# Four engines with instruction orders of their own, tile 1's attention moved into tile 0's FFN, and the last two tiles' attention run as a pair

## What is computed

```python
x = x + linear_attention(layernorm(x))   # 16 heads, silu feature map
x = x + ternary_ffn(layernorm(x))        # 256 -> 1024 (gated silu), 1024 -> 1024 gelu, twice, 1024 -> 256
x = x + softmax_attention(layernorm(x))  # one head of width 256, 512 x 512 scores a tile
x = x + tanh(layernorm(x) @ W @ A1 @ A2 + bias)
```

## Time and profile before

| | |
|---|---|
| median of 3 runs | 2118.21 us (2117.63 to 2120.3) |
| the profiled execution's own time | 2119.35 us |
| its span, first to last instruction | 2117.6 us |
| PE busy | 2008.2 us, 95% of the span, 15484 matmuls |
| PEld, DVE, ACT, POOL busy | 91%, 56%, 40%, 18% |
| granted TensorE clock, mean | 0.991 |

### The profile page before, as it was taken

One profiled execution on the slowest core, in us unless ns is written; L12 is line 12 of the kernel. 1 busy time (PEld: TensorE's weight loads), 2 busy tenths in 40 slices (PEclk: granted clock), 3 DMA queues, 4 the chain that ended last, 5 costly groups with the idle time before them and its releaser, 6 DMA issues.

```text
span 2117.6 us, 37472 instructions
## 1 busy us (share of the span) xinstructions
PE 2008.2 (95%) x15484; PEld 1926.5 (91%) x15484; DVE 1189.6 (56%) x2881; ACT 836.7 (40%) x1538; POOL 373.9 (18%) x347
## 2 busy tenths in 40 slices
PE   6899999999999999999999999999999999999985
PEld 5798999989999998999989999998999989999985
DVE  4555656456565555656456565555656456565544
ACT  2334434344333444434344333444434344333422
POOL 1111211112121011211112121011211112121011
PEclk9999999999999999999999999999999999999997
DMA  9500000000000000000000000000000000000000
GB/s 361 184 3 2 21 1 1 21 1 21 1 21 1 1 21 1 21 1 1 21 1 21 1 21 2 1 21 1 21 1 1 21 1 11 1 11 1 1 11 10
DMA packets 24421, 46.01 MB, mean 22 GB/s; under 512 B 1152, under 2 KB 21376, under 8 KB 24064
## 3 DMA queue, kind: packets, MB, share of 16 engines
q1 hardware_dynamic: 24240, 43.41, 5.8%
HBM read 35.02 MB, written 19.92 MB: 26 GB/s over the span
## 4 chain that ended last, share of the span: by engine, by line
PE 79%; DVE 8%; ACT 5%; DMA 3%; issue 2%; POOL 1%; SPq 0%; DVEq 0%; ACTq 0%; POOLq 0%
PE ffn_fill L857 41%; PE att_fill L818 21%; PE ffn_fill L818 8%; PE ffn_fill L915 6%; PE att_fill L873 2%; DVE whole L585 2%; ACT L786 2%; DMA scratch_h2T<-in_h2T 1%; ACT whole L756 1%; PE att_fill L991 1%; ACT kv_b L786 1%; DVE st L520 1%; DMA scratch_h1T<-in_h1T 1%; POOL act_lo L503 1%; DVE sm L661 1%
## 5 line engine op out<-in xcount | busy, mean ns | idle before, releaser
L857 PE MATMUL ffn_fill<-act_hi,h 128*128 128x256 f32 x4096 | 989.7, 284 | 8.8 <-DVE flag L722 3.3
L857 PE MATMUL ffn_fill<-act_lo,h 128*128 128x256 f32 x4096 | 980.6, 281 | 0.0
L857 PEld LDWEIGHTS ffn_fill<-act_hi,h 128*128 128x128 f32 x4096 | 773.5, 189 | 16.2 <-POOL act_lo L503 6.3
L857 PEld LDWEIGHTS ffn_fill<-act_lo,h 128*128 128x128 f32 x4096 | 774.6, 189 | 3.7
L594 DVE CAST act_hi<-whole 128x512 fp32r<-128x512 f32 x256 | 109.2, 426 | 618.6 <-ACT whole L756 618.6
L756 ACT ACTIVATE whole<-ffn_fill,scales 128x256 f32<-128x256 f32 x512 | 215.1, 471 | 493.0 <-PE ffn_fill L857 491.9
L818 PE MATMUL ffn_fill<-half_hi,w 128*128 128x256 f32 x1024 | 251.4, 287 | 12.8 <-DVE whole L585 9.4
L818 PE MATMUL ffn_fill<-half_lo,w 128*128 128x256 f32 x1024 | 247.2, 282 | 0.0
L503 POOL TENSOR_TENSOR act_lo<-whole,act_hi 128x512 fp32r<-128x512 f32 x128 | 166.8, 1303 | 368.2 <-DVE act_hi L590 367.6
L490 POOL TENSOR_TENSOR rstd_B<-var_eps_B,minus_half 128x2 f32<-128x2 f32 x32 | 22.6, 707 | 1176.7 <-DVE var_eps_B L527 1176.7
L818 PEld LDWEIGHTS ffn_fill<-half_hi,w 128*128 128x128 f32 x1024 | 194.7, 190 | 15.8 <-issue 15.8
(11 more groups left out here) (156 smaller groups left out, 3161.6 us busy)
## 6 DMA issues: line engine op xcount, KB each, us to landing
x<-in_L_attn_x SPq DMA_DIRECT2D x16, 512.0 KB, 3.5
out<-x SPq DMA_DIRECT2D x16, 512.0 KB, 3.0
h<-scratch_h1T SPq DMA_DIRECT2D x1, 4096.0 KB, 18.2
h<-scratch_h2T SPq DMA_DIRECT2D x1, 4096.0 KB, 14.4
w<-scratch_w1T SPq DMA_DIRECT2D x1, 1024.0 KB, 16.0
w<-scratch_w2T SPq DMA_DIRECT2D x1, 1024.0 KB, 19.3
w<-scratch_w3T SPq DMA_DIRECT2D x1, 1024.0 KB, 6.4
rows<-in_rows SPq DMA_DIRECT2D x1, 640.0 KB, 5.7
```

The lines of the kernel that those rows point to most:

```text
L857: last = pe.matmul(two(bank)[:, o, :], view(w), view(moving[:, k, :]), start=k == 0 and o == 0 and half == 0, stop=k == KH - 1 and half == ...
```

## The change

Each engine gets an order of its own for each part, in `PE_ORDERS`, `DVE_ORDERS`, `ACT_ORDERS` and `POOL_ORDERS`; the semaphores' values still come from the one list, from copies of the counters taken at each step. On PE a step can be cut in two pieces (`G0a`, `G0b`), with other steps between them; a piece `a` of a hidden layer does the first half of its contraction. `to_fill` in the U steps is asked for one bank at a time.

`PROLOGUE` loses FOLD, TAKE, WIDE and the checks beyond the first matrix. In `FIRST`, tile 1's whole linear attention and the folding stand inside tile 0's first FFN half. `LAST` and `TAIL` become `END`: tile 15's FFN, nearly alone, and then the softmax attention of tiles 14 (`c:`) and 15 (`d:`) side by side. The `d:` steps have their own buffers, laid over the FFN weights that are done with, own semaphores (`late_...`), and use the `ffn_fill` ring.

On SP, w1 and w2 are bounced first, then tile 1 is loaded, then the raw matrices, which lie no longer in the x slots 1 to 3 and `whole` but in slots 2 and 3 and a buffer `staged`; h1 is bounced behind the landing of w1 and w2; w3 is bounced and landed ahead of h2; each large matrix lands in two DMAs with a semaphore for each half. The stores and loads of x in the steady part are as before, with one semaphore for each slot. The matmuls, and the operations of the other engines, are the same in number and shape.

```diff
 PROLOGUE = steps_from("""
-    a:AST a:ANO a:AB PREP a:T a:AKV0 SCALE a:AKV1 a:AKV2 a:AKV3 a:AS a:AQ a:AM a:AO FOLD0 WIDE
-    n:BST0 n:BNO0 TAKE0 n:BT0 FOLD1 LOOK00 TAKE1 LOOK01 CHECK0 LOOK10 LOOK11""")
+    a:AST a:ANO a:AB PREP a:T a:AKV0 SCALE a:AKV1 a:AKV2 a:AKV3 a:AS a:AQ a:AM LOOK00 a:AO
+    n:BST0 LOOK01 n:BNO0 n:BT0 CHECK0""")
...
+PE_ORDERS = {
+    "FIRST": order_from("""
+    U0 U1 a:T U2a a:AKV0 a:AKV1 a:AKV2 U2b a:AKV3 U3 CHECK1 a:AS a:AQ a:AM FOLD0 G0a a:AOa G0b a:AOb G1 G2
+    FOLD1 CHECK2 G3 H0 H1 H2a CHECK3 H2b H3 BT1 W0 U0 U1 U2 U3 G0 G1 G2 G3 H0 H1 H2 H3 n:BT0 W1"""),
+    "BODY": order_from("""
+    U0 U1 U2 U3a c:T U3b G0a c:CV c:CZ G0b G1a c:CS0 G1b G2 c:CP0 c:CS1 G3a c:CS2 G3b c:CO0 c:CP1 H0a c:CS3
+    H0b c:CO1 c:CP2 H1a c:CO2 c:CP3 H1b H2 c:CO3 H3 BT1 W0 U0a c:T U0b U1 c:CF a:T U2 U3a a:AKV0 a:AKV1
+    a:AKV2 a:AKV3 U3b G0a a:AS a:AQa G0b a:AQb G1 G2 a:AM G3 a:AOa H0 a:AOb H1 H2 H3 n:BT0 W1"""),
+    "END": order_from("""
+    U0 U1 U2 U3 G0 G1 G2 G3 H0 H1 H2 H3 BT1 W0 U0 U1 U2 U3 G0 G1 G2 G3 H0 H1 c:T H2 H3 W1 c:CV c:CZ d:T
+    c:CS0 c:CS1 d:CV c:CP0 d:CZa c:CO0 c:CP1 d:CZb c:CO1 c:CS2 c:CS3 d:CS0 c:CP2 d:CS1 c:CO2 d:CP0 c:CP3
+    c:CO3 d:CO0 d:CS2 d:CP1 d:CO1 d:CS3 d:CP2 d:CO2 d:CP3 c:T d:CO3 c:CF d:T d:CF"""),
+}
+DVE_ORDERS = {
...
+    "BODY": order_from("""
+    c:CST U0 c:CNO U1 c:T U2 U3 c:CQ c:CV c:CZ c:CS0 G0 c:CP0 c:CS1 c:CS2 G1 G2 c:CO0 G3 c:CP1 c:CS3 c:CO1
+    c:CP2 c:CO2 BST1 H0 c:CP3 H1 BNO1 a:AST c:CO3 H2 c:DST H3 BT1 c:DNO W0 c:T a:ANO c:CF U0 a:T U1 a:AKV0
+    a:AKV1 a:AKV2 a:AKV3 U2 U3 a:AS G0 a:AQ a:AM G1 G2 G3 a:AO n:BST0 n:BNO0 H0 H1 H2 H3 n:BT0 W1"""),
...
+ACT_ORDERS = {
...
+    "BODY": order_from("""
+    U0 U1 U2 c:T U3 c:CV c:CZ G0 c:CS0 G1 G2 c:CP0 c:CS1 c:CS2 G3 c:CP1 c:CS3 c:CP2 H0 c:CP3 H1 H2 H3 BT1
+    c:T U0 U1 c:CF a:T U2 a:AKV0 U3 a:AKV1 a:AKV2 a:AKV3 a:AQ G0 a:AM G1 G2 G3 H0 H1 H2 H3 n:BT0"""),
...
+POOL_ORDERS = {
...
+    "BODY": order_from("""
+    c:CST U0 U1 c:CB U2 U3 BST1 a:AST c:DST U0 c:CF U1 a:AB U2 U3 n:BST0"""),
...
+            bounce(0, "w1T", "w2T")
+            sp.dma_start(x[:, 1], x_in[1]).then_inc(x_loaded[1], 16)
...
+            land(0, 0, "w1T", w12[:, 0])
+            land(0, 1, "w2T", w12[:, 1])
+            bounce(1, "h1T")
+            bounce(3, "w3T")
+            sp.wait_ge(w_bounced[1], 16)
+            land(1, 0, "h1T", h1[:, :KH // 2])
+            land(1, 1, "h1T", h1[:, KH // 2:])
+            bounce(2, "h2T")
+            sp.wait_ge(w_bounced[3], 16)
+            land(3, 0, "w3T", w3[:])
+            sp.wait_ge(w_bounced[2], 16)
+            land(2, 0, "h2T", h2[:, :KH // 2])
+            land(2, 1, "h2T", h2[:, KH // 2:])
```

More of the change, by code:

```diff
@@ L21 @@
+from collections import namedtuple
 from contextlib import ExitStack
@@ new lines @@
+    n:BST0 LOOK01 n:BNO0 n:BT0 CHECK0""")
+FIRST = steps_from("""
+    U0 a:AST U1 a:ANO U2 a:T U3 LOOK10 a:AB a:AKV0 a:AKV1 LOOK11 a:AKV2 LOOK12 a:AKV3 LOOK13 CHECK1 a:AS a:AQ
+    G0 a:AM FOLD0 G1 TAKE0 a:AO WIDE G2 LOOK20 LOOK21 FOLD1 TAKE1 G3 LOOK22 LOOK23 CHECK2 LOOK30
+    H0 CHECK3 H1 BST1 BNO1 H2 H3 BT1 W0 U0 U1 U2 U3 G0 G1 G2 G3 H0 H1 n:BST0 n:BNO0 H2 H3 n:BT0 W1""")
+BODY = PLAN
+END = steps_from("""
+    U0 U1 U2 U3 G0 G1 G2 G3 H0 H1 BST1 BNO1 H2 H3 BT1 W0 U0 U1 U2 U3 G0 G1 G2 G3 H0 H1 c:CST c:CNO H2 c:T H3 c:CB W1
+    d:CST c:CQ c:CV c:CZ d:CNO d:T c:CS0 c:CS1 d:CB d:CQ d:CV c:CP0 c:CO0 d:CZ c:CP1 c:CO1 c:CS2 c:CS3
+    d:CS0 d:CS1 c:CP2 c:CO2 c:CP3 c:CO3 d:CP0 d:CO0 c:DST d:CS2 d:CP1 d:CO1 c:DNO d:CS3 c:T d:CP2 d:CO2 d:CP3 d:CO3
+    d:DST c:CF d:DNO d:T d:CF""")
@@ new lines @@
+DVE_ORDERS = {
+    "FIRST": order_from("""
+    a:AST U0 a:ANO U1 a:T LOOK10 LOOK11 a:AKV0 a:AKV1 a:AKV2 LOOK12 LOOK13 a:AKV3 U2 CHECK1 a:AS U3 a:AQ
+    a:AM TAKE0 LOOK20 LOOK21 G0 a:AO WIDE G1 LOOK22 LOOK23 G2 TAKE1 CHECK2 LOOK30 G3 H0 H1 CHECK3 BST1 BNO1
+    H2 H3 BT1 W0 n:BST0 U0 U1 U2 U3 n:BNO0 G0 G1 G2 G3 H0 H1 H2 H3 n:BT0 W1"""),
+    "BODY": order_from("""
+    c:CST U0 c:CNO U1 c:T U2 U3 c:CQ c:CV c:CZ c:CS0 G0 c:CP0 c:CS1 c:CS2 G1 G2 c:CO0 G3 c:CP1 c:CS3 c:CO1
+    c:CP2 c:CO2 BST1 H0 c:CP3 H1 BNO1 a:AST c:CO3 H2 c:DST H3 BT1 c:DNO W0 c:T a:ANO c:CF U0 a:T U1 a:AKV0
+    a:AKV1 a:AKV2 a:AKV3 U2 U3 a:AS G0 a:AQ a:AM G1 G2 G3 a:AO n:BST0 n:BNO0 H0 H1 H2 H3 n:BT0 W1"""),
+    "END": order_from("""
+    U0 U1 U2 U3 G0 G1 G2 G3 H0 H1 BST1 H2 BNO1 H3 BT1 W0 U0 U1 U2 U3 G0 G1 G2 c:CST G3 c:CNO c:T H0 c:CQ H1
+    H2 H3 W1 d:CST c:CV d:CNO c:CZ d:T c:CS0 c:CS1 d:CQ c:CP0 d:CV c:CO0 c:CP1 d:CZ c:CO1 c:CS2 c:CS3 d:CS0
+    c:CP2 d:CS1 c:CO2 c:CP3 d:CP0 c:CO3 d:CO0 d:CS2 d:CP1 c:DST d:CO1 d:CS3 c:DNO d:CP2 d:CO2 d:CP3 c:T
+    d:CO3 d:DST c:CF d:DNO d:T d:CF"""),
+}
@@ L287, in build @@
         raw_wq = gated[:, 0]
[L288 to L295, removed]
+        raw_q, raw_k, raw_v, raw_out = (x[:, 2 + n // 2, 2 * (n % 2):2 * (n % 2) + 2, :] for n in range(4))
@@ L561, in part @@
+                    wait_apart(dve, taken[own.ring][b], n)
+                    statistics(c, own, x[:, slots[who]], stage_of(step), NB)
                 elif kind == "BST":
@@ L843, in ffn_products, with halves, begun, hidden @@
                     emit(lambda ap: ap)
-            def hidden(c, layer, weights, src, j):
-                bank, done = to_fill(pe, c, "ffn_fill", 0)
+            def halves(piece, n):
+                return range(n // 2 if piece == "b" else 0, n // 2 if piece == "a" else n)
+            def begun(c, ring, piece):
+                if piece != "b":
+                    return to_fill(pe, c, ring, 0)
+                b, _ = c.bank(ring, 0)
+                return banks[ring][b], full[ring][b]
+            def hidden(c, layer, weights, src, j, piece):
+                bank, done = begun(c, "ffn_fill", piece)
                 def emit(view):
-                    for k in range(KH):
+                    for k in halves(piece, KH):
                         if j == 0 and k % 2 == 0:
@@ L964, in part @@
                     for k in range(KD):
[L965 to L967 removed]
+                        wait_taken(pe, c, own.ring, c.ago(own.ring, "T", 0, who == "d") + k)
+                    for g in halves(piece, 2):
+                        bank, done = to_fill(pe, c, own.ring, g)
                         for b in range(2):
```

445 lines of the change are left out of this document (243 added, 202 removed).

## The result

The changed kernel takes 2039.08 us, median of 4 runs (2038.69 to 2043.08), against 2119.05 (2117.63 to 2120.3) for the kernel before: the ratio is 0.9627, 95% interval 0.961 to 0.9644. The forecast was 2047. The profiled execution took 2039.22 us, with a span of 2037.5, 80.1 less than before.

A forecast was written before the change was run, and what follows sets the result against it. PE was taken to bound the body, 97% busy at full clock yet losing 6.2 us a pass. Savings of 5.5 (front) + 56 (body) + 10 (end) = 71.5 us gave 2047, range 2027 to 2066 (2027 to 2080 with rivals).

The forecast's parts named there:

- the mechanism: Body: one list serves four engines, so each consumer stands right behind its producer on PE; 6.2 us a pass not work.
- The body: The 14 steady passes: each falls from 126.98 to 123.0 us by new orders, saving 56 us.
- The walk: Following one body pass step by step from U0: 120.8 + 1.6 + 0.65 = 123.0 us, margins 0.2 and 1.5.
- Every gap named as gone: Body PE gaps to vanish: CP1 1.48 us, CO0 0.9, one after CF 0.5, one of 0.36 at the exp chain.
- H0a or U2b: Tightest places in a body pass: margins 1.5 us at H0a, 0.2 at U2b; a new gap there means wrong.
- The normalisation beside POOL: CNO on DVE beside U0's low part on POOL: 2.34 us used; 2.8 at worst, making the body 6 us longer.
- The front: Before the body: moved DMAs and folding start U0 at about 39 and the body at 162, gaining 5.5 us.
- The end: After the body: tile 15's FFN 86 us, then two softmax attentions 76 us; 162 in all, gaining 10 us.
- New waits for old: Rival, body: DVE's margins are absent, PE waits 1 to 3 us a pass; pass about 125.3, time 2079; chance 0.17.
- The clock in the end: Rival, last stage: PE runs its 45 us at 1.2 GHz throughout, time 2080; chance 0.04.
- Slower: Rival, body: DVE holds G1 and G2 behind c:CS2, ACT stops, PE loses 5.6 us a pass; 2125; chance 0.05.
- no change: Rival, whole kernel: the ends lose the body's gain, or gaps are replaced one for one; 2118; chance 0.02.

The follow-up runs named there:

- Experiment 1: Changed kernel, but in the 14 body passes all four engines walk the one list again; front and end stay changed: 2100.62 us.
- experiment 3: Changed kernel, but in PE's body order G3 stands ahead of CP0, CS1, CS2, CO0, CP1: 2055.11 us, one run.
- experiment 8: Changed kernel, but DVE does U1 ahead of normalisation CNO, and PE does U3 whole, then c:T: 2046.22 us, one run.
- Experiment 2: Changed kernel, but no PE step of the body is cut in two; orders of DVE, ACT and POOL unchanged: 2094.4 us, one run.
- experiment 6: Changed kernel, but SP issues h1's bounce ahead of the landing of w1 and w2, as before the change: 2047.47 us, one run.
- experiment 5: Changed kernel, but in tile 0's FFN all four engines walk the new list, without own orders or cuts; same prologue and DMAs: 2055.46 us, one run.
- Experiment 4: Changed kernel, but with the former end: tile 14's attention inside tile 15's FFN, then tile 15's alone, both by the one list: 2052.46 us.
- experiment 9: Changed kernel without PE cuts in the body, and with U3 ahead of the AKV steps on PE, DVE, ACT and POOL: 2118.59 us, one run.
- experiment 12: The changed kernel, unaltered, run again as control on the same chip: 2040.38 us, 5 runs.
- experiment 11: Changed kernel with d:CP1 ahead of d:CS2, d:CP2 ahead of d:CS3 at the end, and LOOK01 behind BNO0 in the prologue: 2033.27 us, 5 runs.

## Why the prediction was right

The time was 8 us under the forecast and inside the range; the mechanism was the one named, and all three terms were too small, so that their errors (1.7, 4.4 and 2.5 us) add up.

- *The body, 56 forecast, 57.7 measured.* The walk gave 123.0 us a pass with one wait of 0.65; the pass is 122.87, with 0.53 at U3b and 0.33 within c:T. From U0 at 0, G1's low part is ready at 35.2 and H0a starts at 36.4 (35.0 and 36.5 in the walk), AKV0's DVE part starts at 76.2 (76.3), AS at 82.0 (82), and CP1's exp has 2.9 us in hand (2.8): the walk held step by step, and not only in its sum. Every gap named as gone is gone, and no new one came at H0a or U2b. Experiment 1 shows that the orders alone do it, experiment 3 that G3 between the attention's steps is 0.8 of the 4.1 us, and experiment 8 that the wait at U3b is DVE's, since it moves with the order of DVE and PE. Experiment 2 adds that orders without cuts, as tried there, keep only 0.4 of the 4.1 in most passes; the prediction didn't price the cuts.
- *The normalisation beside POOL.* I used 2.34 us; it took 2.41. By the Trainium skill, SBUF — State Buffer, section "Who interferes with whom", at its worst it would have been 2.8. I had read the row's delay as a partial block, and that was wrong: a row of four instructions hid it. The view of this line in the window of the four gives the shortest, median and longest:

```profile
L643 DVE TENSOR_SCALAR xn<-x,mv_C,rstd_C x4: 397/398/1440, 654.9 to 656.9; 128x256 f32<-128x256 f32 x4
```

  One instruction, from 654.90 to 656.34, is held until 0.16 us behind the end of POOL's (654.90 to 656.18), and three take 0.40 each, as without POOL. In the kernel before it is the same, with 1.37 and 0.40. So the trace agrees with a block in full of one instruction, and the group's delay of 1.0 us is that one's.
- *The front, 5.5 forecast, 9.9 measured.* The term that was mis-sized is that of the waits from CHECK1 to G3. U0 (39.8 for 39) and CHECK1 (59.2 for 59 to 60) came as said, U0 in part by luck: I had worked it out from the landing of w1 and w2 at about 30 and from FOLD's work leaving the prologue; they landed at 25.3 and 27.8, and what U0 waited for was DVE's chain behind tile 0's attention, as experiment 6 shows with its 5 us in hand. Then I added 3 to 5 us of waits and some half clock to 28 us of work, and G3 came at 89.1, 29.9 us later, rather than 92 to 94. From there to the body it was 68.5 us for 67.6. The sum was also added up wrong: 92 to 94 and 67.6 make 159.6 to 161.6, and I wrote 162, so 0.4 to 2.4 of the 4.4 us missed are that. h2's second half had landed at 80.7, 8 us before G3 starts behind CHECK2. Experiment 6 bears this out from the other side: what delays U0 delays the body by as much. I had not seen how much lies in the order itself: experiment 5 has it at 16.5 us, where the moved DMAs and work alone would have lost 6.6.
- *The end, 10 forecast, 12.5 measured.* The FFN took 85.6 for 86. In the pair, c:CO3, d:CO1 and d:CO2 wait 1.72, 3.13 and 3.13 us for 1.7, 3.1 and 3.1; d:CO3 ends 54.1 us after W1 for 52. Half clock cost 3.4 us (28 matmuls, started 0.19 or 0.09 late each) for the 2.5 counted, 1.5 of it ahead of d:CO3's end and 1.9 in the tail. Without it, it is 52.6 us for 52 up to there, and the term that was too large is the tail: 17.9 us for 19.1 + 2, as c:CF now stands where PE waited 4.5 us for the normalisation, and 2.2 are left of it. Experiment 4 gives the end by itself, 13.4.
- *The rivals.* New waits for old: none behind a step over 0.53 us in a pass, though experiment 9 shows that it was near enough, as one step moved on all four lists, without cuts, made a pass of about 128.5 (half clock behind the gap included; the span is 79.3 us, or 14 x 5.7, over the changed kernel's), which is where the slower case begins. The clock in the end: 0.92, not half throughout. Slower and no change: no.

The Trainium skill, TensorE: Matmul & The Clock Gate, Part 4, says that transposes don't count as busy for the gate. The prediction called them few; they are 56 of the stage's 322 matmuls. Both half-clock stretches of the pair follow transposes and waits, but the rows of the last section show the same transposes and waits once with the fall and once without, so the rule is neither shown nor refuted here.

## What to carry to other kernels

When several in-order engines walk one list, each consumer stands right behind its producer; give every engine its own list and put on the bound engine, between a step and its reader, as many microseconds of other work as the others' chain takes (here 3.5 us for exp and a table load, 2.3 for a split into high and low). Read the waits from starts against the cadence, and check each moved step on all the engines, since a step that stands ahead on one (CF's additions on POOL, 3.0 us in experiment 9) holds back others' products two engines away. The same rule applies once more where two streams run side by side and one ends: there the last steps need their own spacing, which was worth 4.7 us here.

## What the runs showed that was not expected

**The clock falls or not after the same work.** Two windows of the changed kernel, then the same two of experiment 12, which is the same kernel in another execution:

```profile
1968.90:1973.80 4.90, 2.65 (x13) 1.45 (x13) 4.90 (x8) 1.77 (x3) 3.96 (x4) 1.00 0.00 0
1973.80:1977.30 3.50, 3.50 (x11) 2.70 (x10) 1.46 (x4) 0.70 (x1) 0.54 (x1) 0.51 0.00 0
```

```profile
1968.90:1973.80 4.90, 2.66 (x14) 1.63 (x13) 4.90 (x8) 1.77 (x3) 3.96 (x4) 1.00 0.00 0
1973.80:1977.30 3.50, 3.50 (x24) 3.14 (x23) 2.58 (x10) 1.54 (x2) 0.33 (x1) 1.00 0.00 0
```

PE is busy 2.65 of 4.9 us in both, with d:T's transposes and three gaps of 0.7 to 1.4 us; afterwards one has 1.2 GHz for 3.5 us (11 matmuls) and the other 2.4 GHz (24 matmuls). Later it is the other way round: behind the wait of 3.13 us that ends at 2012.56 in the one and 2012.28 in the other, the first goes on at the full clock and the second at half (granted 0.50 from 2012.3 to 2016.0). The pair takes 73.9 us in the one and 75.3 in the other. What decides it the runs don't show, and a single run doesn't settle an edit of 1 to 3 us here. The profiled execution of experiment 11 has neither stretch, which is part of its 7.1 us.

**A wait can cost more than its length.** In experiment 9 a gap of 3.3 us is followed by matmuls 0.43 us apart, and a pass is 2 us longer than in experiment 2, whose gap of 2.2 is followed by matmuls 0.23 apart: the gaps differ by only 1.1 us, and the 16 matmuls of AS and the first five of the queries take 1.6 us more.

**DVE is slower beside POOL in the new order.** DVE's busy time rose from 1189.6 to 1237.9 us at the same 2881 instructions. Two groups make most of it: the reductions of c:CQ went from a mean of 0.42 to 0.91 us, the last multiplication of the AKV steps from 0.52 to 0.77. Both now run more beside POOL:

```profile
662.59 2.90 POOL L613 TENSOR_TENSOR act_lo<-whole,act_hi 128x512 fp32r<-128x512 f32 x2
```

```profile
662.84 1.51 DVE L662 CUSTOM_DVE_ANT_0 kv_b<-xn,rows 128x256 f32<-128x256 f32 x1
```

The first two of c:CQ's four reductions take 1.51 and 1.50 us beside POOL's two instructions, and the last two, behind them, 0.42 each. No step of PE waits for it in this pass, but who writes such an order must give DVE these times where POOL works beside it. ACT lost 44.4 us of busy time, as its table loads fell from 186 to 150: a pass has ten of them rather than twelve.
